# Two mixtures of experts: tokens turned on quarter tiles, and logits, choice and normalisation at other places of the schedule

## The reference

```python
def _L0_ffn_ref(x, gate_w, gate_b, w1, b1, w2, b2, gamma, beta):      # 16 experts, 128 hidden
    gate_logits = x @ gate_w + gate_b
    topk_vals, topk_idx = jax.lax.top_k(gate_logits, 2)
    topk_w = jax.nn.softmax(topk_vals, axis=-1)
    h = jax.nn.relu(jnp.einsum('bsh,ehf->bsef', x, w1) + b1)
    expert_out = jnp.einsum('bsef,efh->bseh', h, w2) + b2
    sel = jnp.take_along_axis(expert_out, topk_idx[:, :, :, None], axis=2)
    y = x + jnp.sum(topk_w[..., None] * sel, axis=2)
    ...                                                               # layer norm of y with gamma, beta
def _L1_ffn_ref(x, Wg, bg, W1, b1, W2, b2):                            # 8 experts, 256 hidden, the same but for
    ...                                                               # a plain sum in place of the norm of y
h = h + _L0_ffn_ref(_layernorm(h, axis=-1), ...)
h = h + _L1_attn_ref(_layernorm(h, axis=-1), ...)
h = h + _L1_ffn_ref(_layernorm(h, axis=-1), ...)
```

## Time and profile before

| what | value |
|---|---|
| median of three runs | 1817.34 us |
| the profiled execution | 1820.9 us, its span 1819.1 us |
| PE busy | 1680.4 us, 92% of the span |
| DVE, ACT, POOL busy | 1251.5, 1040.6, 346.6 us |
| granted TensorE clock, mean over the span | 0.958 of full speed |
| first mixture | about 973 to 1275 us of the span |
| second mixture | about 1534 to 1819 us |

### The profile page before, as it was taken

How to read it: one execution, slowest core, us unless ns; L and a number is a source line. 1 busy time by engine, 2 the same in 40 slices (tenths; PEclk the granted TensorE clock), 3 DMA queues, 4 the chain that set the end, 5 groups by cost and what they waited for, 6 DMA issues and landing times. The chain is left out here.

```text
span 1819.1 us, 50047 instructions
## 1 busy us (share of the span) xinstructions
PE 1680.4 (92%) x20010; PEld 793.1 (44%) x20010; DVE 1251.5 (69%) x3153; ACT 1040.6 (57%) x1963; POOL 346.6 (19%) x325
## 2 busy tenths in 40 slices
PE   7978999999999999999998999999899997999999
PEld 3331222222222222222223555556388985555567
DVE  2559888887888888888734578876777664444432
ACT  1330777776777777777755555554533332565554
POOL 2222000000000000000011056547214344100000
PEclk9975999999999999999979999999999997999999
DMA  5742012121211202120215955671120002352350
GB/s 203 267 98 40 9 37 50 36 50 31 51 37 37 49 25 50 30 49 15 42 32 117 175 119 100 123 143 30 44 73 13 1 2 49 61 100 56 63 101 17
DMA packets 89587, 119.37 MB, mean 66 GB/s; under 512 B 31340, under 2 KB 72374, under 8 KB 87310
## 3 DMA queue, kind: packets, MB, share of 16 engines
q1 hardware_dynamic: 84874, 107.28, 27.1%
q0 software_dynamic: 2992, 8.44, 1.2%
q10 hardware_dynamic: 1492, 0.46, 0.1%
HBM read 97.29 MB, written 18.86 MB: 64 GB/s over the span
## 5 line engine op out<-in xcount | busy, mean ns | idle before, releaser
L870 ACT ACTIVATE b_prob<-b_p_s 128x512 f32<-128x512 f32 x1104 | 570.3, 600 | 262.4 <-PE b_p_s L1060 244.6
L893 DVE TENSOR_REDUCE b_m<-b_p_m 128x1 f32<-128x1024 f32 x512 | 603.8, 1218 | 88.7 <-PE b_p_s L1060 66.9
L1088 PE MATMUL b_p_o<-b_prob,v_all 128*9 128x512 f32 x2304 | 307.6, 617 | 1.0
L1486 ACT ACTIVATE d_hidden<-d_p_z 128x704 f32<-128x704 f32 x192 | 136.1, 756 | 100.9 <-PE d_p_z L1386 98.5
L1486 ACT ACTIVATE n_hidden<-n_p_z 128x704 f32<-128x704 f32 x192 | 135.1, 756 | 87.1 <-PE n_p_z L1386 84.9
L1001 PE MATMUL b_p_m<-b_qk 48*64 48x512 bf16 x856 | 162.8, 442 | 21.8 <-ACT b_prob L870 5.4
L1060 PE MATMUL b_p_s<-b_q,b_k 51*64 51x512 bf16 x1024 | 177.4, 405 | 4.7 <-ACT b_prob L870 4.7
L1060 PE MATMUL b_p_s<-b_qk 51*64 51x512 bf16 x1024 | 177.6, 401 | 2.2 <-ACT b_prob L870 2.2
L848 POOL DMA_DIRECT2D sum_scr<-b_sums x46 | 25.2, 548 | 718.6 <-ACT b_sums L860 653.6
L1386 PE MATMUL d_p_z<-d_xg,d_w 64*64 64x352 f32 x1536 | 139.2, 463 | 10.4 <-DVE d_xg L1619 8.5
L1001 PE MATMUL b_p_m<-b_k,b_q 48*64 48x512 bf16 x800 | 137.1, 392 | 12.2 <-ACT b_prob L870 6.5
(11 more groups left out here) (382 smaller groups left out, 2428.8 us busy)
## 6 DMA issues: line engine op xcount, KB each, us to landing
d_c_wide<-d_c_scr SPq DMA_DIRECT2D x40, 704.0 KB, 11.8
m_x_all<-n_c_scr SPq DMA_DIRECT2D x48, 352.0 KB, 8.4
xt<-in_x SPq DMA_DIRECT2D x16, 1024.0 KB, 10.2
sum_scr<-b_sums POOLq DMA_DIRECT2D x31, 256.0 KB, 2.4
qk_scr<-a_qk_part SPq DMA_DIRECT2D x24, 256.0 KB, 2.9
b_qk<-d_c_scr SPq DMA_DIRECT2D x8, 704.0 KB, 18.3
k_rate<-rate_scr SPq DMA_DIRECT2D x8, 528.0 KB, 4.5
b_qk<-qk_scr SPq DMA_DIRECT2D x56, 66.0 KB
```

The costliest lines, as they stand in the source:

```text
L870: nc.scalar.activation(prob[:, U % PR_RING, 0:w], p_s[:, U % S_RING, 0:w], ACT.Exp, scale=float(D) ** -0.5).then_inc(exp_done, 1)
L893: nc.vector.tensor_reduce(m3[:, x, 0:1], p_m[:, s, :, :].rearrange("p k n -> p (k n)"), axis=AX.X, op=ALU.max).then_inc(rows_free, 1)
L1088: last = nc.tensor.matmul(p_o[32 * i:32 * i + DH + 1, :], v[:, jt, p * QUAD + i, :], prob[:, slot, :], start=(jt == 0), stop=(jt == TILES[ ...
L1486: nc.scalar.activation(own["hidden"][:, n % HR, :, :], own["p_z"][:, n % 2, :, 0:CH], ACT.Relu).then_inc(relu_done, 1)
```

## The change

The doubled copy goes: xn holds the normalised rows once, `double` copies 9 x 63 numbers for each partition in place of 18 x 63, and `turn` makes both halves of the result from the single copy, by four 64x64 matmuls for each tile against quarter identities, into both banks of p_w. `untangle` reads them back from the two banks. The second turn comes two groups behind the first; logits, rank and both parts of choose come one group later; measure, gather and normalise one group sooner. `turn_gates` stays.

```diff
-    TURNS, LOGITS, RANK, CHOOSE, KEEP = (0, 1), 2, 3, (4, 5), 7
+    TURNS, LOGITS, RANK, CHOOSE, KEEP = (0, 2), 3, 4, (5, 6), 7
...
-    xn = sb("xn", [P, NT, 2, D])
+    xn = sb("xn", [P, NT, D])
...
             for k, t in enumerate(TURN_TILES[j]):
-                last = nc.tensor.transpose(own["p_w"][:, k // 4, k % 4 * P:k % 4 * P + P], xn[:, t, :, :].rearrange("p q d -> p (q d)"), g.eye[:])
+                for q, h in HALF_OF:
+                    r = slice(h * D, h * D + D)
+                    last = nc.tensor.matmul(own["p_w"][q * D:q * D + D, h, k * D:k * D + D], xn[r, t, :], g.eye[r, r], start=True, stop=True,
+                                            skip_group_check=True)
...
-            copy(xn[:, :, :, 0:D - 1], normal(b)[:, :, 0:D - 1].unsqueeze(2).to_broadcast([P, NT, 2, D - 1]))\
-                .then_inc(doubled, 1)
+            copy(xn[:, :, 0:D - 1], normal(b)[:, :, 0:D - 1]).then_inc(doubled, 1)
...
-            copy(own["xd"][b % 3][:, tiles[0] * P:tiles[0] * P + len(tiles) * P],
-                 own["p_w"][:, :, :].rearrange("p k n -> p (k n)")[:, 0:len(tiles) * P]).then_inc(misc_free, 1)
+            copy(own["xd"][b % 3][:, tiles[0] * P:tiles[0] * P + len(tiles) * P].rearrange("p (t h n) -> p h t n", h=2, n=D),
+                 own["p_w"][:, :, 0:len(tiles) * D].rearrange("p h (t n) -> p h t n", n=D)).then_inc(misc_free, 1)
...
-                    if answers and i == FIRST_GROUP[B - 1] - 4:
+                    if answers and i == FIRST_GROUP[B - 1] - 5:
...
+                    for b in gating(i, -5):
+                        measure(b)
                     for b in gating(i, -4):
-                        measure(b)
+                        gather(b)
                     for b in gating(i, -3):
-                        gather(b)
-                    for b in gating(i, -2):
                         normalise(b)
```

More of the change, by code:

```diff
@@ L1296, in set_ones @@
             nc.gpsimd.memset(cw[:, NT:, :], 0.0).then_inc(set_up, 1)
-            nc.gpsimd.memset(xn[:, :, :, D - 1:D], 1.0).then_inc(set_up, 1)
+            nc.gpsimd.memset(xn[:, :, D - 1:D], 1.0).then_inc(set_up, 1)
         def rstd_of(b):
@@ L2580, in all_stages @@
             "cen": vn_all[:, 1, :, :],
-            "xn": x_all[:, 4, :, :].rearrange("p f t -> p (f t)")[:, 0:NT * 2 * D].rearrange("p (t q d) -> p t q d", q=2, d=D),
+            "xn": x_all[:, 4, :, :].rearrange("p f t -> p (f t)")[:, 0:NT * D].rearrange("p (t d) -> p t d", d=D),
         }
```

## The result

The changed kernel takes 1849.8 us (median of four runs, 1847.97 to 1862.48), the kernel before 1818.64 in the same comparison (1816.12 to 1834.15). The ratio is 1.0172, 95% interval 1.0143 to 1.0200: slower by some 31 us, where 4 were forecast, outside the range.

A forecast was written before the change was run, and what follows sets the result against it. PE's own queue was taken to bound both mixtures. Terms of -2.0 us in the second and +6.3 in the first sum to +4.3, so 1821.6 us on the median of 1817.34; range 1807 to 1829.

The forecast's parts named there:

- The turns: PE's turns: quarter matmuls in place of transposes save 0.5 us a batch, -3.5 us in each mixture, -7.0 together.
- The sign that I had named for the turns: The forecast for PE's turns is wrong if their intervals are above 0.66 and 0.59 us.
- The choice, in the first mixture: Choice's end on DVE behind add_out and a product: +0.6 us for the last batch only; second mixture +1.8.
- rival D: Slow side: DVE's products meeting POOL's wide operations lose 0.9 us 8 times more, +7, so 1829 us; chance 0.08.
- Normalise ahead of the product: DVE's product waits behind normalise, which waits for POOL: +4.0 us in the second mixture, +9.2 and +1.2 in the first.
- the 1.0 of the first batch: Second mixture's start: PE's wait for a product goes, as DVE's operations ahead of it leave that group: -1.0 us.
- The copy's wait: PE's waits at the first turn for the doubled copy and ACT's queue go: -4.4 us first mixture, -3.3 second.
- The first batch: First mixture's start: rank and measure on DVE stand behind the wait for c_wide's DMA: +3.2 us, bounds 0.5 and 5.
- E: Plain turns on PE cost four times the transposes: +52 us, 1870 or so; chance 0.02.
- C: Normalise on DVE is in time, so all 14.4 us of its lateness goes: 1807.2 us; chance 0.17.
- B: First mixture's lateness is 1.2 us a batch, not 2.3, because PE itself is held: 1817.2 us; chance 0.25.

The follow-up runs named there:

- the places alone: Kernel before with only the new places of the steps, keeping whole turns and doubled copy: 1837.3 us, ratio 1.0092.
- the turns alone: Kernel before with the quarter turns and single copy, all steps kept in their old places: 1853.16 us, ratio 1.0176.
- the run with the early choice: Kernel before with the new places, whole turns and doubled copy, but both parts of the choice in one group, ahead of add_out: 1828.17 us, ratio 1.0060.
- the run of the second mixture alone: Kernel before with quarter turns, single copy and six separately started weight broadcasts in the second mixture only: 1817.51 us, ratio 0.9990.

## Why the prediction was wrong

**The turns: the step that failed.** "Seven batches in each mixture are turned amid groups: -3.5 us each, -7.0 together." The size of the turn itself was right. Where PE had program, the quarter turns took 0.60 and 0.46 in place of 0.67 and 0.59, and in the new places they saved, with the switch, 0.25 + 0.35 = 0.6 a batch (2.97 and 3.21 us from one hidden block to the next, by the places alone 3.22 and 3.56), where 0.5 was forecast. A turn of four in the run of the turns alone, 0.47 to the hidden block behind it:

```profile
1048.15 0.64 PE L1338 MATMUL d_p_w<-eye,d_xn 64*64 64x64 f32 x32
1048.62 1.37 PE L1389 MATMUL d_p_z<-d_xg,d_w 64*64 64x352 f32 x16
1053.92 1.45 PE L1405 MATMUL d_p_y<-d_hidden,d_w 64*64 64x352 f32 x8 [3.94 <-issue]
```

The stop stands behind that block. What the sum left out is the program: it priced 36 matmuls by their time and not by the 126 instructions that they add, in the stretch where program is longest in coming. The sign of this term was wrong: by the turns alone the first mixture grew by 28.3 us, with 15.4 more of gaps and 15.4 lost by the clock, of which some 10 behind stops for program. In the changed kernel 11.9 us of new "issue" waits stand against the forecast -3.5, and 8.5 us of lower clock, for which the sum had no term. The sign that I had named for the turns, their intervals, came out as forecast and could not show this, since the loss is paid in the blocks behind them. There was a hint that I passed over: the kernel before has its "issue" wait of 1.7 us, shown with the result, and its count there is 449 as well. The kernel before was already at the edge.

**The choice, in the first mixture: a term that was missing.** The sum had 0.25 for each batch of the second mixture, 0.6 for the last batch of the first and nothing for its others. In the second it came to one wait of 0.7 us. In the first the places alone show 13.4 us in seven waits, 2.1 to 2.2 in each of the last four. DVE there (start, us, row):

```profile
1106.65 1.01 DVE L1593 TENSOR_TENSOR d_xn_all<-d_xn_all,d_p_w 128x320 f32<-128x320 f32 x2
1107.88 2.45 DVE L1619 TENSOR_TENSOR d_xg<-d_xd,d_c_wide 128x352 f32<-128x352 f32 x2 [0.21 <-PE d_p_z L1386]
1110.24 0.30 DVE L1580 TENSOR_TENSOR d_is<-d_is,d_wt 128x144 f32<-128x144 f32 x1
1110.57 0.31 DVE L1584 TENSOR_TENSOR d_cw<-d_is 128x144 f32<-128x144 f32 x1
```

POOL beside it:

```profile
1107.36 1.17 POOL L1782 TENSOR_TENSOR v_all<-d_xn_all,f_mv 128x576 f32<-128x576 f32 x1
1108.61 1.33 POOL L1784 TENSOR_TENSOR v_all<-v_all,f_mv 128x576 f32<-128x576 f32 x1
```

And PE's turn_gates, which waited for it:

```profile
1111.03 0.34 PE L1354 MATMUL d_p_w<-eye,d_cw 64*64 64x64 f32 x8 [2.09 <-DVE d_cw L1584]
```

The choice's end now stands behind add_out and behind two products, which meet POOL's two wide operations and take 2.45 us for 0.96. The prediction had that very loss in its rows and spent it on rival D, as a general risk, without asking what had been put behind the product.

**Normalise ahead of the product: right in kind.** In the second mixture 4.0 was forecast; after, PE waits 3.7 us in five waits, and the 1.0 of the first batch is gone, as forecast. DVE's rows in one of these groups:

```profile
1611.40 0.70 DVE L1536 BATCH_NORM_AGGREGATE n_mv<-n_st 128x2 f32<-128x6 f32 x9
...
1614.87 0.76 DVE L1545 TENSOR_TENSOR v_all<-v_all,n_rs 128x576 f32<-128x576 f32 x1 [1.69 <-POOL n_rs L1303]
1615.55 1.39 DVE L1621 TENSOR_TENSOR n_xg<-d_xn_all,m_x_all 128x352 f32<-128x352 f32 x3
```

PE's hidden matmul there, and the turn of five behind it:

```profile
1616.21 1.41 PE L1389 MATMUL n_p_z<-n_xg,n_w 64*64 64x352 f32 x16 [0.69 <-DVE n_xg L1621]
...
1618.60 0.79 PE L1338 MATMUL n_p_w<-eye,m_x_all 64*64 64x64 f32 x40
1619.18 1.10 PE L1389 MATMUL n_p_z<-n_xg,n_w 64*64 64x352 f32 x12
```

Gather to normalise's last operation takes 3.47, forecast 3.76, and the turn 0.58. In the first mixture 10.4 was forecast, 2.3 in each of four batches and 1.2. The wait is there and smaller: 1.55 or 1.56 us in each of four batches of the run with the early choice, and 1.55 in three batches of the changed kernel:

```profile
1121.68 0.76 DVE L1545 TENSOR_TENSOR d_xn_all<-d_cen,d_rs 128x576 f32<-128x576 f32 x1 [1.69 <-POOL d_rs L1303]
1122.36 0.95 DVE L1621 TENSOR_TENSOR d_xg<-d_xd,d_c_wide 128x352 f32<-128x352 f32 x2
```

```profile
1123.02 1.42 PE L1389 MATMUL d_p_z<-d_xg,d_w 64*64 64x352 f32 x16 [1.55 <-DVE d_xg L1621]
```

All waits for products together rose by 8.4 with the early choice, and in the changed kernel by 3.6; that PE came to them later there, for other reasons, is argued, not shown.

**The copy's wait** went as forecast, 4.4 and 3.3 us. The first batch cannot be told apart: the first twelve groups took 49.9 us, before 43.8, but with the old places and the turns alone 50.7, and 48.2 in the run of the second mixture alone, whose first mixture is unchanged. **The rivals:** E asked the right question, whether plain turns cost more than transposes, but by PE's time for each, and for the quarter form that stayed refuted. D named POOL, and C and B moved the lateness about; none had PE's program in it.

## What to carry to other kernels

Price a change on PE by its instructions as well as by its time: four small matmuls in place of one are quicker here and bring eight times the program, and it has to come in over DMA engines that other transfers may hold. Look where the long transfers stand before adding instructions there, and take even one "issue" wait in the middle of a block as a sign that an engine is at the edge. When an operation moves in an in-order queue, list what is put ahead of it with the times of that place, not with their times elsewhere.

## What the runs showed of the hardware

A fetch of PE's program is a 16-KB packet that took 0.9 to 1.5 us once it ran (first mixture after). Inside an unbroken broadcast it can be long in coming: one began at 1111.74 and the next at 1129.49, and PE stopped, where the two spacings before, out of the broadcast, were 9.1 and 5.9 us. In ten of the fourteen kernels PE came to an edge at 449 records past 256 for each packet landed, or within four of it, and never beyond. It went on 1.3 to 1.7 us after the landing. Breaking the broadcast into six parts, with PE's progress between them, took the turns alone from 1853.16 to 1821.4 us. And the clock: in the changed kernel's first mixture the granted clock fell to half for 6.8 us behind the stop of 3.17, which so cost about 3.4 more, and for 3.4 us each behind waits of 3.48 and 3.57 and, some 2 us later, behind a stop of 2.53. Behind stops of 2.37 and 2.54 it stayed up. In the profiled execution of the kernel before, whose longest wait there is 1.68 us, it did not fall.
